# A second attention whose scores are three products of two fp32r parts on four row tiles

## The reference, cut

```python
q = rms_norm(x, qn_scale) @ q_w.T + q_b        # k alike, v without the norm
q = q.reshape(B, L, H, HD).transpose(0, 2, 1, 3)   # H = 16, HD = 8
q, k = apply_rotary(q, cos, sin), apply_rotary(k, cos, sin)
scores = jnp.einsum('bhqd,bhkd->bhqk', q, k) * (1.0 / np.sqrt(HD))
weights = jax.nn.sigmoid(scores)
weights = weights / (jnp.sum(weights, axis=-1, keepdims=True) + EPS_RENORM)
attn = jnp.einsum('bhqk,bhkd->bhqd', weights, v)
return attn.transpose(0, 2, 1, 3).reshape(B, L, D) @ o_w.T + o_b
```

## Time and profile before

| | |
|---|---|
| median of 3 runs | 1044.44 us (1044.02 to 1046.89) |
| profiled execution, span from the first to the last instruction | 1041.4 us |
| PE busy | 995.5 us (96%) |
| DVE busy | 834.0 us (80%) |
| ACT busy | 729.9 us (70%) |
| POOL busy | 475.6 us (46%) |
| second attention, from the first score matmul to the last | 702.5 to 976 us |

### The profile page before, as it was taken

How to read it: one execution, slowest core, us unless ns; L and a number is a source line. 1 busy time by engine, 2 the same in 40 slices (tenths; PEclk the granted TensorE clock), 3 DMA queues, 4 the chain that set the end, 5 groups by cost and what they waited for, 6 DMA issues and landing times. The chain is left out here.

```text
span 1041.4 us, 20120 instructions
## 1 busy us (share of the span) xinstructions
PE 995.5 (96%) x5835; PEld 475.4 (46%) x5835; DVE 834.0 (80%) x1874; ACT 729.9 (70%) x939; POOL 475.6 (46%) x483
## 2 busy tenths in 40 slices
PE   8899999999999999999999999999999999999996
PEld 3222222222222235888888887873332333222485
DVE  6889999999999977787888789897666666643677
ACT  2078777787777786555555555568898888899754
POOL 0332514325053725676777677576442244220275
PEclk9999999999999999999999999999999999999998
DMA  6553222131321003344324323443512331230011
GB/s 198 153 186 119 76 76 89 44 117 46 96 78 52 3 2 101 102 128 145 101 91 156 121 90 117 137 137 102 172 65 61 121 119 63 60 122 1 1 31 52
DMA packets 73981, 97.04 MB, mean 93 GB/s; under 512 B 12669, under 2 KB 42237, under 8 KB 73533
## 3 DMA queue, kind: packets, MB, share of 16 engines
q1 hardware_dynamic: 73928, 96.40, 29.7%
HBM read 68.18 MB, written 27.79 MB: 92 GB/s over the span
## 5 line engine op out<-in xcount | busy, mean ns | idle before, releaser
L741 DVE TENSOR_REDUCE a_nmax<-a_ps_f 128x1 f32<-128x512 f32 x512 | 320.1, 683 | 20.2 <-PE a_ps_f L579 19.7
L497 ACT ACTIVATE a_prob<-a_ps_s 128x1024 f32<-128x1024 f32 x256 | 251.7, 1023 | 77.8 <-PE a_ps_s L646 76.5
L1367 ACT ACTIVATE a_prob<-a_ps_s 128x1024 f32<-128x1024 f32 x256 | 244.4, 1026 | 28.0 <-PE a_ps_s L1419 26.7
L2187 POOL TENSOR_TENSOR moe_hl<-moe_hid,moe_hh 128x512 fp32r<-128x512 f32 x134 | 173.9, 1303 | 84.3 <-ACT moe_hh L2068 84.2
L579 PE MATMUL a_ps_f<-a_ks,a_qs 48*128 48x512 bf16 x512 | 157.9, 386 | 11.8 <-DVE a_nmax L741 4.3
L2058 ACT ACTIVATE moe_ps<-moe_ps 128x512 f32<-128x512 f32 x128 | 74.5, 582 | 111.5 <-PE moe_ps L1981 110.7
L1432 PE MATMUL a_ps_o<-a_prob,a_va 128*32 128x512 f32 x1024 | 136.4, 605 | 1.4 <-DVE a_turned_o L1547 0.5
L659 PE MATMUL a_ps_o<-a_prob,a_va 128*32 128x512 f32 x1024 | 136.4, 605 | 0.5 <-ACT a_prob L497 0.4
L646 PE MATMUL a_ps_s<-a_qs,a_ks 51*128 51x512 bf16 x512 | 132.5, 381 | 1.7 <-ACT a_prob L497 1.5
L579 PEld LDWEIGHTS a_ps_f<-a_ks,a_qs 48*128 48x128 bf16 x512 | 39.7, 93 | 192.2 <-DVE a_nmax L741 162.2
L2109 DVE TENSOR_TENSOR moe_prod<-moe_cw,moe_ps 128x512 f32<-128x512 f32 x128 | 87.2, 681 | 27.4 <-PE moe_ps L1981 26.7
(11 more groups left out here) (302 smaller groups left out, 1640.1 us busy)
## 6 DMA issues: line engine op xcount, KB each, us to landing
moe_cw<-r_weights SPq DMA_DIRECT2D x256, 128.0 KB, 2.9
parts_q<-a_parts SPq DMA_DIRECT2D x48, 256.0 KB, 2.5
parts_k<-a_parts SPq DMA_DIRECT2D x48, 256.0 KB, 2.5
a_qs<-parts_q SPq DMA_DIRECT2D x126, 96.0 KB, 2.4
a_ks<-parts_k SPq DMA_DIRECT2D x126, 96.0 KB, 2.5
a_xt<-in_x_t SPq DMA_DIRECT2D x8, 256.0 KB, 2.8
out_x<-g_X SPq DMA_DIRECT2D x7, 256.0 KB, 2.3
moe_wg<-in_wg SPq DMA_DIRECT2D x1, 1088.0 KB, 6.6
```

The costliest lines, as they stand in the source:

```text
L497: nc.scalar.activation(prob[:, u % PSLOTS, :, :], ps_s[:, u % 2, :, :], ACT.Exp, scale=float(P) ** -0.5).then_inc(exp_done, 1)
L741: nc.vector.tensor_reduce(nmax[:, half_no, h % 2, col:col + 1], ps_f[:, bank, :], AX.X, ALU.max, negate=True).then_inc(max_done, 1)
L1367: nc.scalar.activation(prob[:, u % PSLOTS, :, :], ps_s[:, u % 2, :, :], ACT.Sigmoid, scale=float(HD) ** -0.5).then_inc(exp_done, 1)
L2187: nc.gpsimd.tensor_tensor(hl[:, part_at(j), :], hid[:, hid_at(j), :], hh[:, part_at(j), :], ALU.subtract).then_inc(hl_done, 1)
```

## The change

q and k are split into two parts in fp32r instead of three in bf16: the first part is the rounded value, the second the rest (`split_in_two`). A score is the sum of three part products (first with first, first with second, second with first), which makes a stack of 24 rows a head. Four heads lie in one column of the stack tile, at partitions 0, 32, 64 and 96 (`quarter_rows`), so that the two matmuls of an even unit use the row tiles 0 and 1 and those of an odd unit the tiles 2 and 3. The order of the columns of the q and k weights changes with it (`heads` in `layouts`).

`write_terms` writes three rows of terms in two DMAs, and `read_terms` reads 24 rows and the columns of half of the heads with one DMA; a batch has four writes and 16 loads. The loads are counted by halves: PE waits at units 0 and 16 for eight loads each. In `Head` the second and third step of the split fall away. The first attention and the other stages keep their code.

```diff
 QKR = PAIRS * HD
 MXR = QKR + PARTS
 HALF = P // 2
+TERMS = 3
+QTR = P // HG
+FQKR = TERMS * HD
 PAIR_DIMS = HD // 2
 UN = 2
 NU = NG * NT * (HG // UN)
...
     for i in halves:
         src = bass.AP(tensor=scratch.tensor, offset=(i * HH + 2 * grp) * T, ap=[[H * T, QKR], [1, 2 * T]])
         sp.dma_start(dst[HALF * i:HALF * i + QKR, 2 * grp:2 * grp + 2, :], src).then_inc(done, 16)
+
+
+def quarter_rows(tile, h, n_rows):
+
+    return tile[QTR * (h % HG):QTR * (h % HG) + n_rows, h // HG, :]
+
+
+def write_terms(sp, scratch, parts, n, done):
+
+    dst, src = scratch.rearrange("r p t -> p r t"), parts.bitcast(F32)
+    if n == 0:
+        sp.dma_start(dst[:, 0:2, :], src[:, n, 0:1, :].broadcast_to([P, 2, T])).then_inc(done, 16)
+        sp.dma_start(dst[:, 2:3, :], src[:, n, 1:2, :]).then_inc(done, 16)
+    else:
+        sp.dma_start(dst[:, 0:2, :], src[:, n, 0:2, :]).then_inc(done, 16)
+        sp.dma_start(dst[:, 2:3, :], src[:, n, 0:1, :]).then_inc(done, 16)
+
+
+def read_terms(sp, scratch, dst, g0, count, done):
+
+    for i in range(HG):
+        src = bass.AP(tensor=scratch.tensor, offset=(i * NG + g0) * T, ap=[[H * T, FQKR], [1, count * T]])
+        sp.dma_start(dst[QTR * i:QTR * i + FQKR, g0:g0 + count, :].bitcast(F32), src).then_inc(done, 16)
+
+
+def split_in_two(eng, ops, src, parts, k, split, parts_done, zero):
+
+    ops.tensor_tensor(parts[:, 0, :], src, zero, ALU.add).then_inc(split, 1)
+    eng.wait_ge(split, k + 1)
+    ops.tensor_tensor(parts[:, 1, :], src, parts[:, 0, :], ALU.subtract).then_inc(parts_done, 1)
 
 
 def split_in_parts(eng, ops, src, rest, parts, k, split, parts_done, zero=None):
...
     e, place = {}, first
     for name, shape, dt in (("xb", [P, NT, P], F32), ("xr", [P, NT, P], F32), ("ms", [P, NT], F32), ("rr", [P, NT], F32),
                             ("xrh", [P, T], F32R), ("xrl", [P, T], F32R), ("turned", [P, 2, T], F32),
-                            ("qk", [P, 2, T], F32), ("parts", [P, 2, PARTS, T], BF16)):
+                            ("qk", [P, 2, T], F32), ("parts", [P, 2, 2, T], F32R)):
         e[name] = nc.alloc_sbuf_tensor_at("a1_" + name, shape, dt, offset=place)
         place += -(-math.prod(shape[1:]) * (2 if dt == BF16 else 4) // 32) * 32
     for i, name in enumerate(("qs0", "ks0")):
-        e[name] = nc.alloc_sbuf_tensor_at("a1_" + name, [P, HH, T], BF16, offset=wide + i * NB * T * 4)
+        e[name] = nc.alloc_sbuf_tensor_at("a1_" + name, [P, NG, T], F32R, offset=wide + i * NB * T * 4)
     home = nc.sbuf_base
     for name, shape, dt in (("wh", [P, 2, P], F32R), ("wl", [P, 2, P], F32R), ("xt0", [P, T], F32),
                             ("rest", [P, T], F32)):
...
     e["ln0"] = layernorm_buffers(ctx, nc, "a0")
     e["y"] = ctx.enter_context(nc.sbuf_tensor("moe_y", [P, NT, P], F32))
     e["ln"] = layernorm_buffers(ctx, nc, "moe")
-    e["scratch"] = [[nc.dram_tensor(f"parts1_{n}{i}", [PAIRS, P, T], BF16).ap() for i in range(2)] for n in "qk"]
+    e["scratch"] = [[nc.dram_tensor(f"parts1_{n}{i}", [TERMS, P, T], F32).ap() for i in range(2)] for n in "qk"]
     for name in ("w_scaled", "x_step", "x_pow", "xr_done", "xrh_done", "f_done", "f_taken", "rope_done", "split",
                  "parts_done", "parts_out"):
         e[name] = sem(name)
     e["head"] = [sem(f"head_{n}") for n in "qk"]
-    e["stack_in"] = [[sem(f"stack_in{i}{j}") for j in range(NG)] for i in range(2)]
+    e["stack_in"] = [[sem(f"stack_in{i}{j}") for j in range(2)] for i in range(2)]
     return e
 
 
-PARTS_C, OUT_C, R_C, FN = 2, 6 * 16, 1, 4
+PARTS_C, OUT_C, R_C, FN = 2, 4 * 16, 1, 4
 HEAD_RMS, HEAD_POW, HEAD_SCALE, HEAD_TURN, HEAD_QK, HEAD_X = 0, 2, 3, 6, (13, 17), 23
 HEAD_SUM, HEAD_PARTS = (17, 23), (24, 27)
 NEXT_RMS, NEXT_POW, NEXT_SCALE = 28, 31, 32
...
             act.wait_ge(e["f_done"], 4)
             nc.scalar.activation(e["xt0"][:, :], self.ps_t, ACT.Copy).then_inc(e["f_taken"], 1)
         for n in range(2):
-            hi = 2 * n
             if k == HEAD_SUM[n] + 1:
                 act.wait_ge(e["rope_done"], n + 1 + R_C)
-                nc.scalar.activation(e["parts"][:, n, hi, :], e["qk"][:, n, :], ACT.Copy).then_inc(e["head"][n], 1)
-            if k == HEAD_PARTS[n] + 1:
-                act.wait_ge(e["head"][n], 2)
-                nc.scalar.activation(e["parts"][:, n, 1, :], e["rest"][:, :], ACT.Copy).then_inc(e["head"][n], 1)
+                nc.scalar.activation(e["parts"][:, n, 0, :], e["qk"][:, n, :], ACT.Copy).then_inc(e["head"][n], 1)
 
     def vector_first(self, dve, k):
...
                                         ALU.add).then_inc(e["rope_done"], 1)
             if k == HEAD_PARTS[n]:
                 dve.wait_ge(e["head"][n], 1)
-                if n:
-                    dve.wait_ge(e["parts_done"], 1 + PARTS_C)
-                nc.vector.tensor_tensor(e["rest"][:, :], e["qk"][:, n, :], e["parts"][:, n, hi, :],
-                                        ALU.subtract).then_inc(e["head"][n], 1)
-            if k == HEAD_PARTS[n] + 2:
-                dve.wait_ge(e["head"][n], 3)
-                nc.vector.tensor_tensor(e["parts"][:, n, lo, :], e["rest"][:, :], e["parts"][:, n, 1, :],
+                nc.vector.tensor_tensor(e["parts"][:, n, 1, :], e["qk"][:, n, :], e["parts"][:, n, 0, :],
                                         ALU.subtract).then_inc(e["parts_done"], 1)
 
     def vector(self, dve, k):
...
 
     for n in range(2):
         sp.wait_ge(e["parts_done"], 2 * b + n + 1 + PARTS_C)
-        write_pairs(sp, e["scratch"][n][p], e["parts"], n, e["parts_out"])
+        write_terms(sp, e["scratch"][n][p], e["parts"], n, e["parts_out"])
 
 
 def load_stacks(sp, e, dsts, b, p):
 
     sp.wait_ge(e["parts_out"], OUT_C * (b + 1) + OUT_C)
-    for grp in range(NG):
+    for half in range(2):
         for n, dst in enumerate(dsts):
-            read_pairs(sp, e["scratch"][n][p], dst, grp, e["stack_in"][p][grp])
+            read_terms(sp, e["scratch"][n][p], dst, half * NG // 2, NG // 2, e["stack_in"][p][half])
 
 
 def attention1(ctx, nc, g, c, e, xh, xl, ff):
...
             def s2(b, p, u):
 
                 grp, kt, pair = u // (2 * NT), u // 2 % NT, u % 2
-                if u % (2 * NT) == 0:
-                    pe.wait_ge(stack_in[p][grp], 32 * (b - p) + 64)
+                if u % (NU // 2) == 0:
+                    pe.wait_ge(stack_in[p][grp // 2], 64 * (b - p) + 128)
                 if not (is_first(b) and u < 2):
                     pe.wait_ge(exp_done, NU * b + u - 1 + EXP_C)
                 for i in range(UN):
                     h = grp * HG + pair * UN + i
-                    mm = nc.tensor.matmul(ps_s[:, u % 2, i, :], stack_rows(ks[p], h, QKR)[:, kt * P:(kt + 1) * P],
-                                          stack_rows(qs[p], h, QKR), start=True, stop=True)
+                    mm = nc.tensor.matmul(ps_s[:, u % 2, i, :], quarter_rows(ks[p], h, FQKR)[:, kt * P:(kt + 1) * P],
+                                          quarter_rows(qs[p], h, FQKR), start=True, stop=True)
                 mm.then_inc(s2_done, 1)
 
             def pv(b, p, e):
...
 
                 pool.wait_ge(parts_out, OUT_C * b + OUT_C)
                 pool.wait_ge(rope_done, 2 * b + n + 1 + R_C)
-                split_in_parts(pool, nc.gpsimd, qk[:, n, :], rest[:, :], parts[:, n, :, :], 2 * b + n, split,
-                               parts_done, g["zero"][:, :].broadcast_to([P, T]))
+                split_in_two(pool, nc.gpsimd, qk[:, n, :], parts[:, n, :, :], 2 * b + n, split, parts_done,
+                             g["zero"][:, :].broadcast_to([P, T]))
 
             def units(b, p, u0, u1, qk_on, front, back, tail):
                 if u0 == 0 and tail:
...
     r["wd"] = np.ascontiguousarray(down.reshape(FF, P, P).transpose(1, 0, 2))
     q, k, v, o = (np.asarray(i[f"L1_attn_{n}_w"]).T for n in "qkvo")
     dims = dims % PAIR_DIMS * 2 + dims // PAIR_DIMS
+    heads = at % NG * HG + at // NG
     order = heads * HD + dims
     rows = np.zeros((P, NO, P), dtype=np.float32)
     for h in range(H):
```

More of the change, by code:

```diff
@@ L1178, in vector_first @@
         for n in range(2):
-            hi, lo = 2 * n, 2 - 2 * n
             if k - 1 - HEAD_QK[n] in range(3):
@@ L1304, in attention1 @@
         w, bqk, norm_scale, vb, ob, cos, sin = (c[n] for n in ATT1_SHAPES)
-        xb, xr, ms, rr, xrh, xrl, wh, wl, turned, qk, rest, parts = (
-            e[n] for n in ("xb", "xr", "ms", "rr", "xrh", "xrl", "wh", "wl", "turned", "qk", "rest", "parts"))
+        xb, xr, ms, rr, xrh, xrl, wh, wl, turned, qk, parts = (
+            e[n] for n in ("xb", "xr", "ms", "rr", "xrh", "xrl", "wh", "wl", "turned", "qk", "parts"))
         xn = xb
@@ L1310, in attention1 @@
         xt = [e["xt0"], sb("xt1", [P, T])]
-        qs = [e["qs0"], sb("qs1", [P, HH, T], BF16)]
-        ks = [e["ks0"], sb("ks1", [P, HH, T], BF16)]
+        qs = [e["qs0"], sb("qs1", [P, NG, T], F32R)]
+        ks = [e["ks0"], sb("ks1", [P, NG, T], F32R)]
         va = [sb(f"va{i}", [P, SLOT + NT * H * CT]) for i in range(2)]
```

(2 more changed lines are left out.)

## The result

| | before | after |
|---|---|---|
| median of 4 runs, us | 1044.23 (1043.94 to 1046.89) | 1059.06 (1058.59 to 1062.16) |
| ratio, with its 95% interval | | 1.0145 (1.0114 to 1.0175) |
| profiled execution, span, us | 1041.4 | 1056.7 |
| ACT busy, us | 729.9 | 731.2 |
| POOL busy, us | 475.6 | 441.1 |

A forecast was written before the change was run, and what follows sets the result against it. Neither PE nor ACT was full; their hand-over of scores and sigmoids in the second attention was taken as the bound. 154 units x 0.11 = 16.9 us on 1044.4 gave 1061 us; forecast range 1052 to 1071 us, chance 0.64.

The forecast's parts named there:

- the price of a unit: Second attention: two score matmuls in fp32r take 0.43 us against 0.32, 0.11 us more, from load and stream.
- lone unit: Two score matmuls and one sigmoid, its scores not back to back with another's on PE; forecast 0.43 us against 0.32.
- The count: Second attention: 154 units have their extra time on the path, 5 x 20 + 3 x 18, costing 16.9 us.
- my twenty units: Fourth batch: 20 of 32 units, followed on the timeline, were said to lie on the path, each paying 0.11 us.
- plain round: Four units without projections or other matmuls put in: two of four on the path, so 16 a batch, 18 with projections.
- What was counted at nothing: GpSimd's shorter split, operations ACT and DVE lose, SyncE's queue and DMAs: all off the path, 0 us.
- The cover: First batch's stacks land by 701.7 us, scores begin at 702.5; 1.9 us once if that lead were gone.
- Loads hidden, four tiles together: Rival at score matmuls: extra load falls away, three free pairs a batch give 5 us; 1039 us, chance of faster 0.09.
- No change: Rival: load costs little and four tiles give as little, as ACT releases pairs singly; 1044 us, chance 0.11.
- bound of 0.8 us for four tiles: Paired units on disjoint row tiles: nothing counted, at most 8 x 0.10 = 0.8 us gained.
- Four tiles act as two: Rival: back-to-back pairs run in turn, 0.665 us instead of 0.53; 1062 us, inside the forecast, no separate chance.
- Row tiles take turns: Rival: fp32r row tiles alternate even within a unit, 53 us more, 1097 us; chance 0.10 for above 1073 us.

The follow-up runs named there:

- e1: Changed kernel with its layout kept, but parts, scratch and stacks in bf16 instead of fp32r (coarser scores); 1042.35 us, 0.9979 of the kernel before.
- e3: Kernel before, each score matmul preceded by one of the same operands over the first 256 columns, which the real one overwrites; 1063.49 us, ratio 1.0189.
- e4: Changed kernel with POOL's split put back to four operations and PE waiting for both halves of the stacks at unit 0; 1059.28 us.
- e2: Changed kernel with heads placed so both units of a pair use the same two row tiles instead of all four; 1061.39 us, ratio 1.0162.
- e6: Kernel before, each score matmul preceded by one over 16 columns, adding a second stationary load per row tile; 1047.81 us, ratio 1.0038.

## Why the prediction was right

**The mechanism and the price of a unit** came out as forecast. The load was to be near 189 ns and is 181, a lone unit 0.43 us and is 0.43 (0.110 more, against 0.11). A sigmoid that waits was to start 0.62 us after its scores; one of them, of the pair 10 and 11 in the fourth batch, is this row of ACT's timeline, 0.63 us behind 824.43:

```profile
825.06 1.94 ACT L1389 ACTIVATE a_prob<-a_ps_s 128x1024 f32<-128x1024 f32 x2 [0.78 <-PE a_ps_s L1441]
```

That the type makes it is shown by e1, which takes nothing away but the type (and with it half the bytes of the DMAs): load 90 ns, lone unit 0.32, loss gone. That most of it is the load, and 0.02 us the stream, is read from the rows, where the prediction had 0.085 and 0.025. That a lone unit of this length costs about this much, whatever made it long, is shown by e3. The 24 rows and the row tile of 32 had no row in the trace before; the value from the fp32r load of 128 rows was the right neighbour.
**The count is the term that was mis-sized**, 154 units against 144. The way to see it is to line up the unit starts of the two timelines in the fourth batch, each from unit 0 of its own kernel (differences are rounded from the trace's nanoseconds):

| start of unit | before, us | after, us | difference | gained since the row above |
|---|---|---|---|---|
| 1 | 0.91 | 0.91 | 0.00 | |
| 4 | 4.96 | 5.27 | 0.32 | 1, 2, 3 |
| 8 | 9.28 | 9.91 | 0.63 | 4, 6, 7 |
| 10 | 11.90 | 12.63 | 0.73 | the pair 8, 9: 0.09 |
| 14 | 16.31 | 17.25 | 0.94 | 10, 13 |
| 16 | 17.99 | 18.94 | 0.95 | 14: 0.01 |
| 17 | 18.99 | 19.96 | 0.97 | 16: 0.02 |
| 18 | 20.31 | 21.39 | 1.08 | 17 |
| 24 | 26.31 | 27.71 | 1.40 | 18, 21, 22 |
| 28 | 30.44 | 32.16 | 1.72 | 24, 25, 26 |
| next 0 | 34.57 | 36.61 | 2.04 | 28, 29, 30 |

Eighteen of my twenty units cost 0.10 to 0.11 us each. Units 14 and 16 cost 0.01 and 0.02. Behind unit 16 PE's transposes begin 0.42 us after the scores before (824.15, 824.57) and 0.43 after, so that something other than the scores was holding them in the kernel before; it is DVE's copy of x, as the row of their loads says:

```profile
824.56 0.42 PEld L1401 LDWEIGHTS a_ps_f<-g_ident,a_xb 128*128 128x128 f32 x4 [0.32 <-DVE a_xb L1500]
```

That copy covers unit 14 as well, which comes ahead of the same transposes. In the third and the fifth batch unit 14 does cost 0.10 and 0.11 us (its sigmoid starts 0.51 us after its scores before and 0.62 after), and unit 16 gives 0.10 and 0.09 back: the two together cost nearly nothing there too. In the fourth batch unit 14 costs nothing by itself, because its sigmoid already started 0.60 us after its scores in the kernel before; what held it there no row names. In e1 it starts after 0.51; that kernel gains 0.10 us there and gives it back at unit 16. I had named both as lone units by their place in the order, and not asked what ended last behind them. On the other side, the pair 8 and 9 ahead of the v product, for which I counted a gain or nothing, cost 0.09: its second unit is released late, and its longer load is hidden only in part (0.63 against 0.54 in the rows above). The eighteen together gave 1.92 us, and with 0.03 and 0.09 that is the 2.04 by which the batch grew, where I had 2.2. Sigmoid to sigmoid, the first to the eighth batch grew by 2.07, 1.97, 2.03, 2.04, 2.04, 2.03, 1.91 and 1.71 us; for the first, seventh and eighth I had 1.98 each, taken from a plain round and not followed unit by unit. Together 15.8 us against 16.9. The medians of the runs differ by 14.8, so 1061 us was forecast and 1059.06 measured; the 1.0 us between 15.8 and 14.8 is inside the spread of the runs and has no cause shown.

**ACT's idle time** grew by 13.2 us (28.0 to 41.2) and not by 17. The stage's 15.8 us show in the group's busy time as well (244.4 to 246.9), although a sigmoid takes the same 1026 ns: sigmoids that follow each other at once overlap a little in the rows, and those that wait don't. 13.2 + 2.5 is 15.7. I had set the idle time equal to the extra time, and the view doesn't measure that.

**What was counted at nothing** was nothing. POOL lost 4.9 us a batch where 4.4 were forecast, and e4 shows that adding 29.1 us to it moves no time. No wait of PE for a stack appeared, and the first scores don't wait for stacks that are issued 6.3 us earlier. The cover that I had named there held.

**The rivals.** "Loads hidden, four tiles together" had its breakeven at 0.03 us more a unit; it got 0.110. "No change" needed 0.02. The first rival's other half, that four tiles run together, was right, as the pair of 0.44 us shows, but e1 shows what it is worth when the load is short: 0.67 us of stage and 1.5 us of time, and not the 5 us that the rival gave it. The prediction's own bound of 0.8 us for four tiles covers the stage. "Four tiles act as two" is wrong for this kernel, and e2 shows that it would have been hardly slower had it been true, as the prediction said (1061.39 us against 1062). "Row tiles take turns" would have shown 0.66 us for a lone unit; it is 0.43.

## What to carry to other kernels

Where two engines hand work to each other through few buffers, price the time from the start of a hand-over to what it releases, at each place in the order, and ask at each place what ends last; an operand type that saves work on paper but lengthens the first load of stationary data is paid at every lone hand-over. Independent tiles pay only where two pieces of work are free at the same moment and the engine's time behind them is on the path, so count those places before counting the tiles. To find which units carry a loss, line up the starts of the same work in both timelines: the differences rise in steps, and each step is a cost with its place.

## What the runs showed of the hardware that was not expected

- Row tiles of 32 run four at a time in fp32r and in bf16: two units, four matmuls, hold PE 0.44 us in fp32r. In bf16 it is the 0.32 us of one unit, as PE's timeline of e1_bf16_four_tiles shows for units 10 and 11:

```profile
821.94 0.40 PE L1441 MATMUL a_ps_s<-a_qs,a_ks 24*128 24x512 bf16 x4
822.26 1.06 PE L1454 MATMUL a_ps_o<-a_prob,a_va 128*32 128x512 f32 x8
```

- The fp32r load of 24 rows and 128 columns takes 181 ns, nearly that of 128 rows (189) and twice the 90 ns of bf16: the rows hardly count, the type does.
- A second load into the same row tiles is taken up 0.01 us after the first, and costs 0.025 us instead of its 0.09 to 0.10 (e6).
